# A chunked attention and mixture-of-experts kernel on Trainium2: the value product ahead of the scores in each attention step

## The chip, the cores and the metric

One NeuronCore of one Trainium2 chip runs the whole program. The metric is the device time of one execution in microseconds (us). Before the change the median of three runs is 1189.48 us (1186.12 to 1189.49).

## The reference, cut to what matters

Tokens are 2 batches of 2048 rows of 256 numbers. A layer norm with a per-batch shift and scale feeds an attention with 16 heads of 64 and a window of 128 keys; its output is gated and added. A second modulated layer norm feeds a router and eight experts.

```python
h = layernorm(x) * (1 + ca) + sa
q, k, v = split(h @ Wqkv)                      # 16 heads of 64
scores = (q @ k.T) / 8                         # key j seen by query i if i-127 <= j <= i
x = x + ga * (softmax(scores) @ v).reshape(...) @ Wout
h = layernorm(x) * (1 + cb) + sb
x = x + gb * experts_top2_capacity_640(h)      # relu(h W1 + b1) W2 + b2, gated
```

## The kernel before, in words

**Tiling.** The 4096 tokens are eight chunks of 512 (c = 0 to 7), a chunk is four tiles of 128. In a chunk the attention is cut into 16 units: a pair of heads j times half of the chunk's tiles (two tiles). A unit's scores, probabilities and transposed probabilities are four 128x128 blocks each.

**The pipeline.** A unit passes through five stages on four engines, and each engine has its own hand-written program; only semaphores tie them together:

- `scores` (L568, matmuls on L585), on TensorE, into one of two PSUM tiles `score`;
- on VectorE (DVE) `softmax_step` (L991): `merge` (L967, the window's mask, L976), `invert_sum` (L982, L984), `row_max` (L978, L980), `normalise` (L986, L988), where the sum and the normalisation belong to the unit before; between them ScalarE (ACT) takes the exponentials (`exponentials`, L817, L822);
- `transposes` (L591, L596) on TensorE into the one PSUM tile `pt`, copied by ACT (`copy_probT`, L826, L830);
- `split_keys` (L1230) on GpSimd (POOL), two masked copies (L1237, L1239) into one of two buffers `probT_split`;
- `weighted_values` (L599, L616 and L623) on TensorE, the value product of a pair of heads into the one PSUM tile `pv`. When both halves of the pair are there, ACT takes the high part out (`attn_high`, L832, L836) and DVE the low part (`attn_low`, L999, L1001). In the last chunk this is done for every unit by itself, half as wide (L844, L1096).

**The step.** A chunk is a loop over i = 4 to 19 on every engine. In step i TensorE takes the scores of unit i, the value product of unit i-4, the transposes of unit i-2, and then the projections of q, k or v for the next chunk (`project_qk`, six matmuls of 512 columns on L548; `project_v`, L562). Steps 12, 13, 14 and 16 have a v projection beside the q or k one. Units above 15 belong to the next chunk. Step 5 also has the transposes of the layer norm of chunk c+2. Step 12 has the router's logits (L688), step 15 its counts (L702). After step 19 come four v projections and the output projection (L639). Chunk 6 leaves the projections of pairs 5 to 7 and some of v to chunk 7, so its steps 14 to 19 have none; chunk 7 does them two at a time in its steps 4 to 6, and has no scores after step 15.

**Who waits for whom on TensorE.** `scores` of unit i waits for the exponentials of unit i-2 (`exp_done`), which read the same PSUM tile, and on the first half of a pair for the copy of its q and k out of PSUM (`gen_free`). `weighted_values` of unit u waits for both masked copies (`cur_ready`, `prev_ready`), and as it writes the one tile `pv`, for `attn_low` of the pair before (`attn_lo`), on the first unit of each pair, that is in even steps:

```python
if c == LAST:
    at_least(pe, attn_lo, PAIRS * c + u)
elif part == 0:
    at_least(pe, attn_lo, PAIRS * c + j)
```

On DVE `attn_low` stands at the head of an even step, behind the whole `softmax_step` of the odd step before; on ACT `attn_high` stands in that odd step behind its exponentials. POOL also does the router's modulation: `route_scale` in step 6 (L356), `route_shift` in step 7 (L360), `route_low` (L365) in step 9, each behind that step's `split_keys`; the first waits for DVE's L227 of step 6. From step 16 on it issues the scatters (L1248). In chunks 1 to 6 DVE has `route_top` (L1042 to L1059) after the softmax of step 13, and `route_slots` (L1073 to L1090) behind `attn_low` in step 16.

Of the kernel before, what the change touches and what calls it, by code (L numbers as in the profile page):

```python
# [45 lines left out]
def build(nc, x_in, wqkv_in, wout_in, gate_w, gate_b, w1_in, b1_in, w2_in, b2_in, c_in, wmod_in, out):  # L46
# [22 lines left out]
    with whole:  # L69
# [57 lines left out]
        with attn_stack:  # L127
# [128 lines left out]
            def projections_at(c, i):  # L256

                if c == LAST:
                    return LATE.get(i, [])
                v_tiles = {12: 0, 13: 1, 14: 2, 16: 3}  # L260
                names = [("qk"[i % 2], (i - LAG) // 2)] + ([("v", 0, v_tiles[i])] if i in v_tiles else [])
                return [n for n in names if c != LAST - 1 or n not in LATE_NAMES]
# [14 lines left out]
            def route_at(c):  # L277
                return LAST_AT if c == LAST else ROUTE_AT
# [215 lines left out]
            if True:  # L494
# [27 lines left out]
                def attention_tensor(pe):  # L522
                    def claim(c, name):
                        bank, before = group(c, name)
                        at_least(pe, gen_free[bank], before)
                        return gen[bank], gen_full[bank]
# [64 lines left out]
                    def transposes(c, h):  # L591
                        u = H * c + h
                        pe.wait_ge(norm_ready, u + 1)
                        at_least(pe, probT_ready, u)
                        for b in range(TILES):
                            mm = pe.transpose(pt[:, b, :], prob[:, h % 2, b, :], identf[:])  # L596
                        mm.then_inc(pt_done, 1)
# [108 lines left out]
                    def project(c, name):  # L706
                        cc = c - 1 if c == LAST else c
                        if name[0] == "v":
                            project_v(cc, name[1], [name[2]])
                        else:  # L710
                            project_qk(cc, name)

                    def chunk(c, first, last):
                        at = route_at(c)
                        for i in STEPS:
                            if i < H or not last:
                                scores(c, i)
                            weighted_values(c, i - 4)
                            if i - 2 < H or not last:
                                transposes(c, i - 2)  # L720
                            if last:
                                for name in projections_at(c, i):
                                    project(c, name)
                            if last and i == at["turn"]:
                                route_transposes(c)
                            if not first and i == at["logits"]:
                                route_logits(c)
                            if not first and i == at["counts"]:
                                route_counts(c)
                            if last and i == OUT_AT:  # L730
                                pe.wait_ge(attn_lo, PAIRS * c + PAIRS)
                                early, early_full = claim(c, ("out", 0))
                                project_out_tile(early, 0, range(PAIRS))
                            if last and i == OUT_AT + 1:
                                project_out_tile(early, 1, range(PAIRS)).then_inc(early_full, 1)
                            if last and i == EARLY_AT["turn"]:
                                route_part_transposes(NC)
                            if last and i == EARLY_AT["logits"]:
                                route_logits(NC)
                            if i == 5 and c + 2 < NC:  # L740
                                ln_transposes(c, c + 2, "lnT")
                            if not last:
                                for name in projections_at(c, i):
                                    project(c, name)
                        if not last:
                            for name in projections_after(c):
                                project(c, name)
                            project_out(c)
                            return
                        pe.wait_ge(attn_lo, PAIRS * c + H - 1)  # L750
                        late = [claim(c, ("out", t - 1)) for t in (2, 3)]
                        for t in (2, 3):
                            project_out_tile(late[t - 2][0], t, range(PAIRS - 1))
                        pe.wait_ge(attn_lo, PAIRS * c + H)
                        for t in (2, 3):
                            project_out_tile(late[t - 2][0], t, [PAIRS - 1]).then_inc(late[t - 2][1], 1)
                        route_counts(NC)
                        route_part_transposes(NC + 1)
                        route_logits(NC + 1)
                        route_counts(NC + 1)  # L760
# [850 lines left out]
```

## Time and profile before

| | us |
|---|---|
| median of three runs | 1189.48 |
| lowest, highest | 1186.12, 1189.49 |
| the profiled execution's own time | 1186.38 |
| its span | 1184.7 |
| TensorE busy | 1099.4 |
| VectorE busy | 770.2 |
| ScalarE busy | 661.8 |
| GpSimd busy | 501.2 |

The span runs from the first to the last instruction; 1.7 us of the execution's time lie around it. A chunk of the attention takes 85 us of it, the eight chunks lie between 67 and 722 us, and the experts take the rest. In rows of the timeline the first number is the start of a group of equal instructions and the second the time to the end of the last; TensorE's instructions overlap, so what a part of a step costs is read from start to start.

### The profile page before, as it was taken

The page shows a single profiled execution, that of the slowest core. Times are in us where ns is not written, and L with a number is a line of the kernel's source. Part 1 is how long each engine was busy: PE and PEld are TensorE (multiplying, and loading weights), DVE is VectorE, ACT ScalarE, POOL GpSimd, SP SyncE. Part 2 cuts the span into 40 slices and gives each one's busy share as a digit, 9 for nine tenths or more (in the row PEclk, how much of TensorE's full clock was granted, in tenths as well). Part 3 has the DMA queues.
Part 4 walks back from the last instruction along what each step waited for, and adds up shares of the span by engine and source line. Part 5 has one row for each costly group of instructions (what it writes and reads, how often), then busy time and mean ns, then how long its engine had stood idle before and what let it go on. Part 6 is the DMA issues. An engine that isn't in the chain of part 4 may idle for free.

```text
span 1184.7 us, 25298 instructions
## 1 busy us (share of the span) xinstructions
PE 1099.4 (93%) x9508; PEld 720.3 (61%) x9508; DVE 770.2 (65%) x1687; ACT 661.8 (56%) x1876; POOL 501.2 (42%) x555
## 2 busy tenths in 40 slices
PE   6899999999999999999999874599999999999996
PEld 3355655655655655655656553275858677585865
DVE  6566487586586587585675675376666667666654
ACT  3377566476476476476473753456373746637361
POOL 2134254464364365265344554525243433524342
PEclk9999999999999999999999987699999999999998
DMA  9653000110100011000001021734253444535000
GB/s 330 106 169 132 2 23 20 38 31 16 41 20 26 30 20 37 19 19 31 20 19 50 2 91 36 200 97 94 87 99 113 85 130 112 135 108 84 22 20 9
DMA packets 119627, 80.60 MB, mean 68 GB/s; under 512 B 82770, under 2 KB 110550, under 8 KB 119252
## 3 DMA queue, kind: packets, MB, share of 16 engines
q1 hardware_dynamic: 108756, 57.46, 18.4%
q0 software_dynamic: 10752, 21.54, 6.5%
q8 instruction: 76, 1.25, 0.4%
q14 instruction: 43, 0.35, 0.1%
HBM read 39.49 MB, written 33.78 MB: 62 GB/s over the span
## 4 chain that ended last, share of the span: by engine, by line
PE 76%; DVE 7%; issue 6%; POOL 6%; ACT 3%; DMA 1%; SPq 0%; POOLq 0%; ACTq 0%; DVEq 0%
PE up L1444 18%; PE down L1459 18%; PE gen L548 10%; PE gen L639 6%; PE gen L562 6%; PE score L585 5%; PE pv L616 4%; PE pt L596 4%; PE pv L623 3%; ACT prob L822 2%; POOL probT_split L1237 2%; POOL h L356 1%; POOL probT_split L1239 1%; DVE prob L988 1%; PE gen L647 1%
## 5 line engine op out<-in xcount | busy, mean ns | idle before, releaser
L1503 ACT ACTIVATE hid<-up,b1T 128x512 f16<-128x512 f32 (+1 forms) x192 | 124.4, 648 | 195.3 <-PE up L1444 193.6
L1444 PE MATMUL up<-xT,w 128*128 128x512 f16 (+1 forms) x1152 | 213.1, 346 | 17.2 <-DMA xT<-slot_inputs 17.2
L1459 PE MATMUL down<-w,hid 128*128 128x256 f16 x1920 | 212.2, 273 | 0.0
L1237 POOL TENSOR_SCALAR_AFFINE_SELECT probT_split<-probT 128x512 f32<-128x512 f32 x128 | 98.3, 768 | 262.5 <-ACT probT L830 257.2
L1459 PEld LDWEIGHTS down<-w,hid 128*128 128x128 f16 x1920 | 187.8, 98 | 23.5
L548 PE MATMUL gen<-hT,big 128*128 128x512 f16 x768 | 186.8, 383 | 5.5 <-DVE hT L1197 2.9
L822 ACT ACTIVATE prob<-score,negmax 128x128 f32<-128x128 f32 x512 | 180.9, 374 | 8.0 <-DVE negmax L980 7.9
L1444 PEld LDWEIGHTS up<-xT,w 128*128 128x128 f16 x1152 | 113.4, 98 | 112.6 <-issue 21.1
L1404 POOL DMA_INDIRECT out<-y,tail x80 | 79.9, 998 | 218.5 <-DVE y L1560 206.1
L1531 DVE TENSOR_TENSOR hid<-hid 128x512 f16<-128x512 f32 (+1 forms) x192 | 115.4, 607 | 82.1 <-ACT hid L1505 66.1
L830 ACT ACTIVATE probT<-pt 128x512 f32<-128x512 f32 x128 | 76.6, 598 | 101.3 <-PE pt L596 101.1
L976 DVE COPY_PREDICATED score<-above,score 128x512 f32<-128x512 int32 x112 | 77.2, 690 | 84.3 <-PE score L585 84.3
L1505 ACT ACTIVATE hid<-up,b1T 128x512 f32<-128x512 f32 (+1 forms) x192 | 124.8, 650 | 0.0
L548 PEld LDWEIGHTS gen<-hT,big 128*128 128x128 f16 x768 | 74.3, 99 | 75.9 <-issue 4.7
L585 PE MATMUL score<-k,q 64*64 64x192 f32 (+2 forms) x2048 | 111.6, 331 | 8.0 <-ACT prob L822 5.8
L822 ACT ACTIVATION_READ_ACCUMULATOR prob<-score,negmax 128x1 f32 x512 | 109.9, 215 | 0.0
L616 PE MATMUL pv<-probT_split,v 128*64 128x256 f32 x512 | 84.5, 408 | 24.0 <-issue 7.7
L988 DVE TENSOR_TENSOR prob<-prob,rinv 128x512 f32<-128x512 f32 x128 | 105.4, 823 | 0.0
L1393 POOL DMA_INDIRECT kept<-out,tail x80 | 85.2, 1065 | 47.6 <-issue 30.2
L585 PEld LDWEIGHTS score<-k,q 64*64 64x64 f32 x2048 | 64.9, 133 | 59.5 <-issue 57.3
L562 PE MATMUL gen<-big,hT 128*128 128x512 f16 x384 | 91.3, 384 | 0.0
L1239 POOL TENSOR_SCALAR_AFFINE_SELECT probT_split<-probT 128x512 f32<-128x512 f32 x128 | 86.5, 676 | 0.0
(143 smaller groups left out, 1484.7 us busy)
## 6 DMA issues: line engine op xcount, KB each, us to landing
big<-in_L_ffn_W SPq DMA_DIRECT2D x16, 1024.0 KB, 7.3
slot_inputs<-empty_row SPq DMA_DIRECT2D x80, 129.5 KB, 2.5
out<-x SPq DMA_DIRECT2D x8, 512.0 KB, 2.9
x<-in_L_attn_x SPq DMA_DIRECT2D x1, 3072.0 KB, 22.1
q<-in_L_attn_Wqkv SPq DMA_DIRECT2D x2, 1024.0 KB, 8.0
kept<-out,tail POOLq DMA_INDIRECT x80, 4.8
out<-y,tail POOLq DMA_INDIRECT x80, 2.4
x<-in_L_attn_x SPq DMA_DIRECT2D x2, 512.0 KB, 8.8
```

The lines of the kernel that those rows point to most:

```text
L548: mm = pe.matmul(dst[:], wqkv[:, kd, a, col:col + P], hT[:, cn % 2, kd, b, :], start=(n == 0), stop=(n == 5))
L562: mm = pe.matmul(dst[:], hT[:, cn % 2, kd, a, s * P:(s + 1) * P], wqkv[:, kd, b, 2 * INNER + half * 512:2 * INNER + (half + 1) * 512], sta ...
L585: mm = pe.matmul(dst[lo:lo + HALF, 2 * hd + i, first:lo + P + HALF], q[r:r + DH, j, b * P + lo:b * P + lo + HALF], k[r:r + DH, j, b * P + ...
L616: mm = pe.matmul(pv[r:r + DH, 2 * part * P:(2 * part + 2) * P], v[:, 2 * part + 1, h * DH:(h + 1) * DH], probT_split[:, par, 2 * hd:2 * hd ...
L822: mm = act.activation(prob[:, h % 2, b, :], score[h % 2][:, b, P:], ACT.Exp, bias=negmax[:, h % 2, b:b + 1], accum_out=rowsum[:, h % 2, b: ...
L988: dve.tensor_tensor(prob[:, h % 2], prob[:, h % 2], rinv[:, h % 2, :].unsqueeze(2).to_broadcast([P, TILES, P]), ALU.mult)\
L1237: pool.affine_select(out=probT_split[:, h % 2, :, 1], in_=probT[:, h % 2], pattern=[[0, TILES], [1, P]], compare_op=ALU.is_ge, fill=zero, ...
L1444: mm = pe.matmul(bank[:, 0:size], w1[:, par, kd, a, ft * P:(ft + 1) * P], xT[:, par, b * KD + kd, lo:lo + size], start=(i == 0), stop=(i = ...
L1459: mm = pe.matmul(down[n][:, s, :], hid[:, ft, a, t * P:(t + 1) * P], w2[:, par, ft, b, :], start=(i == 0), stop=(i == 3 * FT - 1))
L1503: act.activation(hid[:, ft, 0, lo:lo + size], up[ft % 4][:, 0:size], ACT.Relu, scale=1 / W_SCALE, bias=bias).then_inc(hid_hi, 1)
L1505: act.activation(hid32[:, k_ % 4, 0:size], up[ft % 4][:, 0:size], ACT.Relu, scale=1 / W_SCALE, bias=bias).then_inc(up_out, 1)
L1531: dve.tensor_tensor(hid[:, ft, 1, lo:lo + size], hid32[:, k_ % 4, 0:size], hid[:, ft, 0, lo:lo + size], ALU.subtract).then_inc(hid_ready, 1)
```

## The change: what it does, and the diff

In the step loop of TensorE's program the call for the value product of unit i-4 moves ahead of the call for the scores of unit i. The programs of the other four engines, the waits, the tiles and the data are the same.

```diff
--- before.py
+++ after.py
@@ -713,9 +713,9 @@
                     def chunk(c, first, last):
                         at = route_at(c)
                         for i in STEPS:
+                            weighted_values(c, i - 4)
                             if i < H or not last:
                                 scores(c, i)
-                            weighted_values(c, i - 4)
                             if i - 2 < H or not last:
                                 transposes(c, i - 2)
                             if last:
```

TensorE's order before, from the scores of an odd step in the middle of a chunk to the value product of the next, even step (each helper's first matmul carries its waits):

```order
L585 MATMUL score<-k,q 64x192 [waits exp_done]
L585 MATMUL score<-k,q 64x192 x7
L616 MATMUL pv<-probT_split,v 64x256 [waits cur_ready,prev_ready]
L616 MATMUL pv<-probT_split,v 64x256
L623 MATMUL pv<-probT_split,v 64x128 x4
L596 MATMUL pt<-identf,prob 128x128 [waits probT_ready,norm_ready]
L596 MATMUL pt<-identf,prob 128x128 x3
L548 MATMUL gen<-hT,big 128x512 [waits gen_free1]
L548 MATMUL gen<-hT,big 128x512 x5
L585 MATMUL score<-k,q 64x192 [waits exp_done,gen_free0,gen_free1]
L585 MATMUL score<-k,q 64x192 x7
L616 MATMUL pv<-probT_split,v 64x256 [waits attn_lo,cur_ready,prev_ready]
```

And with the change, from the same scores to the same value product:

```order
L585 MATMUL score<-k,q 64x192 [waits exp_done]
L585 MATMUL score<-k,q 64x192 x7
L596 MATMUL pt<-identf,prob 128x128 [waits probT_ready,norm_ready]
L596 MATMUL pt<-identf,prob 128x128 x3
L548 MATMUL gen<-hT,big 128x512 [waits gen_free1]
L548 MATMUL gen<-hT,big 128x512 x5
L616 MATMUL pv<-probT_split,v 64x256 [waits attn_lo,cur_ready,prev_ready]
```

Between the odd step's scores and the wait on `attn_lo` stood two groups of value products, transposes, projections and scores; now transposes and one projection stand there, since the odd step's value product is done before its scores and the even step's scores come behind the wait.

The last chunk on TensorE before, steps 11 and 12, where every value product waits on `attn_lo`:

```order
L596 MATMUL pt<-identf,prob 128x128 [waits probT_ready,norm_ready]
L596 MATMUL pt<-identf,prob 128x128 x3
L585 MATMUL score<-k,q 64x192 [waits exp_done]
L585 MATMUL score<-k,q 64x192 x7
L616 MATMUL pv<-probT_split,v 64x256 [waits gen_free0,attn_lo,gen_free1,cur_ready,prev_ready]
L616 MATMUL pv<-probT_split,v 64x256
L623 MATMUL pv<-probT_split,v 64x128 x4
```

The same place with the change:

```order
L596 MATMUL pt<-identf,prob 128x128 [waits probT_ready,norm_ready]
L596 MATMUL pt<-identf,prob 128x128 x3
L616 MATMUL pv<-probT_split,v 64x256 [waits gen_free0,attn_lo,gen_free1,cur_ready,prev_ready]
L616 MATMUL pv<-probT_split,v 64x256
L623 MATMUL pv<-probT_split,v 64x128 x4
L585 MATMUL score<-k,q 64x192 [waits exp_done]
L585 MATMUL score<-k,q 64x192 x7
```

The scores of unit 12 went from ahead of this wait to behind it. The orders of DVE and ACT are the same before and after.

## Rows read from the trace of the kernel before

**Rows 1.** The page, part 1: busy us (share of span) xinstructions, each engine.
```profile
PE 1099.4 (93%) x9508; PEld 720.3 (61%) x9508; DVE 770.2 (65%) x1687; ACT 661.8 (56%) x1876; POOL 501.2 (42%) x555
```

**Rows 2.** Busy us by stretch, chunk 3: window, length, then each engine's busy (x instructions).
```profile
319.00:404.00 85.00, 82.60 (x814) 51.16 (x808) 59.05 (x145) 52.01 (x180) 41.96 (x48) 1.00 0.09 26
```

**Rows 3.** Waits in total, of L616 and of L1001: us, times, longest us.
```profile
PE pv L616 <- POOL probT_split L1239: 7.2, 14, 1.0
PE pv L616 <- DVE attn L1001: 4.9, 8, 1.2
...
DVE attn L1001 <- ACT attn L836: 0.2, 1, 0.2
```

**Rows 4.** Timeline of TensorE, chunk 3, step 9 and start of 10: start, us.
```profile
339.53 0.88 PE L585 MATMUL score<-k,q 64*64 64x192 f32 x16
340.58 0.65 PE L616 MATMUL pv<-probT_split,v 128*64 128x256 f32 x4 [0.18 <-POOL probT_split L1239]
...
341.60 0.66 PE L596 MATMUL pt<-identf,prob 128*128 128x128 f32 x4
342.10 1.46 PE L548 MATMUL gen<-hT,big 128*128 128x512 f16 x6
343.48 0.88 PE L585 MATMUL score<-k,q 64*64 64x192 f32 x16
344.30 0.65 PE L616 MATMUL pv<-probT_split,v 128*64 128x256 f32 x4
```

**Rows 5.** Timeline of VectorE, the same steps 9 and 10.
```profile
340.48 0.70 DVE L976 COPY_PREDICATED score<-above,score 128x512 f32<-128x512 int32 x1 [0.51 <-PE score L585]
341.66 0.18 DVE L984 RECIPROCAL rinv<-rowsum 128x4 f32<-128x4 f32 x1 [0.49 <-ACT prob L822]
...
342.33 0.68 DVE L988 TENSOR_TENSOR prob<-prob,rinv 128x512 f32<-128x512 f32 x1
342.93 0.68 DVE L1001 TENSOR_TENSOR attn<-pv,attn 128x512 f16<-128x512 f32 x1
...
345.42 0.68 DVE L976 COPY_PREDICATED score<-above,score 128x512 f32<-128x512 int32 x1
346.01 0.17 DVE L984 RECIPROCAL rinv<-rowsum 128x4 f32<-128x4 f32 x1
```

**Rows 6.** Timeline, chunk 3, steps 7 and 8: the chain over POOL.
```profile
332.58 2.36 POOL L356 TENSOR_TENSOR h<-h,modrow 128x1024 f32<-128x1024 f32 x1 [3.86 <-DVE h L227]
335.94 0.63 POOL L1239 TENSOR_SCALAR_AFFINE_SELECT probT_split<-probT 128x512 f32<-128x512 f32 x1
336.62 0.65 PE L616 MATMUL pv<-probT_split,v 128*64 128x256 f32 x4 [0.60 <-POOL probT_split L1239]
```

**Rows 7.** Timeline, chunk 3, steps 11 to 14.
```profile
350.14 1.52 DVE L988 TENSOR_TENSOR prob<-prob,rinv 128x512 f32<-128x512 f32 x1
...
352.47 0.65 PE L616 MATMUL pv<-probT_split,v 128*64 128x256 f32 x4 [0.68 <-POOL probT_split L1237]
...
359.40 0.18 DVE L984 RECIPROCAL rinv<-rowsum 128x4 f32<-128x4 f32 x1 [0.49 <-ACT prob L822]
...
362.83 0.68 DVE L1001 TENSOR_TENSOR attn<-pv,attn 128x512 f16<-128x512 f32 x1
...
363.66 0.65 PE L616 MATMUL pv<-probT_split,v 128*64 128x256 f32 x4 [0.51 <-DVE attn L1001]
```

**Rows 8.** Timeline of TensorE, chunk 6, step 18.
```profile
628.45 0.65 PE L616 MATMUL pv<-probT_split,v 128*64 128x256 f32 x4 [1.15 <-DVE attn L1001]
```

**Rows 9.** Timeline of TensorE, chunk 7, steps 5 and 12.
```profile
652.56 0.88 PE L585 MATMUL score<-k,q 64*64 64x192 f32 x16 [0.73 <-issue]
687.68 1.12 PE L616 MATMUL pv<-probT_split,v 128*64 128x256 f32 x4 [2.80 <-issue]
```

**Rows 10.** Busy us by stretch; the third last column is the granted clock.
```profile
628.00:632.00 4.00, 2.55 (x34) 1.79 (x36) 3.08 (x7) 2.49 (x13) 3.40 (x5) 1.00 0.16 57
686.00:688.00 2.00, 0.32 (x2) 0.32 (x4) 1.93 (x14) 0.10 (x2) 0.05 (x1) 0.79 1.09 377
```

## The prediction

> **What bounds the kernel now.** I began with the page's busy times: TensorE is busy for 93% of the span [rows 1]. The busy times by stretch say that this holds inside the attention too: 82.6 of 85 us in chunk 3, at the full granted clock [rows 2]. So a step of the attention lasts as long as TensorE's own work, and what matters is how near the other engines are behind. The table of waits answers that: the value product L616 waits 14 times for POOL and 8 times for DVE, 1.2 us at most [rows 3]. They are short, but they show two chains that only just arrive. The timeline then gives the lengths, all from start to start [rows 4]: scores S 0.82 (343.48 to 344.30), value product V 1.02 (340.58 to 341.60), transposes T 0.50, one projection Q 1.38 us. A plain step is 3.72 us. (A measurement of this kernel can tell 0.3%, 3.6 us, from no change.)
>
> **The change, part by part.** It removes and adds no instruction on any engine, and no DMA; each of 124 pairs of S and V is swapped. TensorE's work stays the same, so without waits it costs 0. The swap has two effects on waits. V comes 0.82 us earlier against a producer that has not moved. And S comes 1.02 us later in its step, with everything that DVE does behind it.
>
> *The even steps, a plain pair.* V of an even step waits for `attn_low`, which stands behind the odd step's whole softmax on DVE. From S of the odd step the chain is [rows 5]: 0.95 to the merge (339.53 to 340.48), 0.59 merge to reciprocal (345.42 to 346.01), 0.67 reciprocal to normalisation, 0.60 to `attn_low`, 0.68 for that, and 0.15 from its end to TensorE's start (363.51 to 363.66) [rows 7]: 3.64 us. Before, the reciprocal came later, 2.13 us after S, since it waited for ACT's exponentials; that made 4.23 us. TensorE covered it with S, V, T, Q and the next S, 4.54 us: 0.3 us of slack, no wait. Now the exponentials stand where they stood in the step while S comes 1.02 later, so the merge sets the reciprocal and the chain is 3.64. But TensorE has only S, T and Q in front of the wait, 2.70 us. **The wait is 0.94 us**, and nothing takes it back, as the next such chain starts behind it. Behind the waiting V stand S of its own step, T and Q; DVE idles for S. If this wait were gone, POOL would be late next.
>
> *Step 8.* V waited 0.60 us for POOL's copies, which were late because L356 began only behind DVE's L227 [rows 6]. L227 moves with the softmax of step 6: merge-bound, the reciprocal comes 1.02 + 0.95 + 0.59 = 2.56 us after the step's start instead of 2.13, 0.43 later, and POOL with it. V begins 0.43 later than before, and S, which was done during the wait, now comes behind: 0.43 + 0.82, **1.2**. Step 9's V waits for POOL as before (0.18, [rows 4]): 0.
>
> *Step 12.* On DVE the normalisation of step 11 takes 1.52 instead of 0.68 us [rows 7], beside a POOL instruction. The chain is 3.64 + 0.84, TensorE's cover 2.70: a wait of 1.8 where 0.68 was [rows 7]. (The row names POOL, but those copies belong to the next unit; `attn_low` ended just before.) **1.1.**
>
> *Step 14.* The router's small instructions lie between reciprocal and `attn_low`: 359.40 to 363.51, 4.11 us [rows 7]. The chain from S is 0.95 + 0.59 + 4.11 + 0.15 = 5.80. The cover is S, T, Q and a v projection of 1.3: 4.0. Wait 1.8, where 0.51 was, and S used to be done inside it: 1.8 less 0.51 is **1.2 to 1.3**, as the chain also lost 0.58 of waiting for ACT, V's 1.02 now lying ahead of S. I take 1.24.
>
> *Steps 10, 16, 18.* Plain pairs at 10 and 18: 0.94 each. Ahead of step 16 the counts (0.36 us) cover some: 0.58. Step 6 has the layer norm's transposes as cover: 0.
>
> Chunks 1 to 5: 1.2 + 0.94 + 1.1 + 1.24 + 0.58 + 0.94 = 6.0 us each, 30.2. **Chunk 0** has no router: 0.94 before steps 8, 10, 16 and 18, and step 12's 1.1: 4.9. **Chunk 6**: 1.2 + 0.94 + 0.94 + 1.24 up to step 14. From there it has no projections, and waits of up to 1.15 us already [rows 8]; walking the pairs in the same way gives +1.3 and +0.5, and 0.6 back at step 19, where the scatters on POOL set the time: 5.5. **Chunk 7** hands over in every step. Its steps 4 to 7 come out even: S waited 0.73 us for the copy of its k [rows 9], three times, and now V lies in that wait. Steps 8, 9 and 11 cost 1.5, 0.7 and 0.7. In step 12 V waits 2.80 us [rows 9] and S, issued ahead of that wait until now, comes behind: 1.8, and its softmax then holds the V of step 13: 1.1. At step 16 the long DVE chain starts from an S 1.02 later: 1.0. With 0.3 won before: 6.5. This walk is the roughest term.
>
> Sum 30.2 + 4.9 + 5.5 + 6.5 = **47 us**. The experts come after and are only shifted: 0, unless the shift moves the last DMA. On the profiled execution's 1186.38 us this gives 1233.5; the median of the runs is 3.1 above it, so 1236.5.
>
> *A cost the trace does not show*: the new neighbours on TensorE (V behind a projection, S behind V, T behind S). The nearest rows are the overlaps of neighbours now, 0.06 to 0.08 us (S lasts 0.88, the next starts after 0.82; Q 1.46 and 1.38) [rows 4]. Three seams a step in 64 odd steps (even ones wait anyway): at most 15 us more or less. I take 0, since the tile shapes change as often as before, and keep both ends.
>
> **The rivals.**
> *Only the waits already there grow.* If DVE's chain of a plain pair fits after all (it would have to be 0.94 us shorter), the terms of 0.94 and 0.58 fall away: 12.3 in chunks 1 to 5, 3.8 in chunk 0, 1.9 in chunk 6, about 18. Time: 1218. For it: the chain had 0.3 of slack, so my two lengths differ by small numbers. Against: the five spans of which it is made would have to be read too long together.
> *Hidden.* Every V finds its inputs at the step's start: 1189.5. The four waits of a chunk that the trace already has speak against it.
> *Faster.* One mechanism: V 0.82 us earlier lets ACT's L836 and so `attn_low` end earlier, and the waits on DVE go. It decides if L1001 waits for L836. It did so once, for 0.2 us [rows 3]; L1001 is held by DVE's own queue. Price if true: 4.9 us of L1001's waits [rows 3], step 12's five of 0.68 [rows 7], three of 0.73 [rows 9]: 10.5 us, 1179.
> *The clock falls.* After the wait of 2.80 us in step 12 of chunk 7 the value product took 1.12 instead of 0.65 us [rows 9], and the granted clock of that stretch was 0.79 on the way to half, the 1.2 GHz level [rows 10]. In chunk 6, with TensorE idle for 1.4 of 4 us in pieces, it stayed at 1.00, 2.4 GHz [rows 10]. My new waits of 1.8 to 1.9 us at steps 8, 12 and 14 lie between the two. If each cost a V and an S at half rate, 1.8 us, 20 times, the time is 1236.5 + 36 = 1272. The Trainium skill (TensorE: Matmul & The Clock Gate, Part 1) has the half rate as the gate's default that only activity lifts; by that rule this rival is the danger in a change that only adds idle time, and the trace agrees in its 2.80 us wait. I hold it unlikely, since dense work stands on both sides of each wait.
>
> **How the numbers follow.** Forecast 0.74, only existing waits 0.13, clock 0.06, hidden 0.04, faster 0.03. The range 1212 to 1258 holds the forecast with most of its seam costs (15 either way) and 7 more for the walks of chunks 6 and 7, and the second case; the clock, hidden and faster cases are left out. Slower by over 0.3%: 0.93; within: 0.04; faster: 0.03.
>
> **What would show it.** In the profile of the changed kernel L616's waits for DVE L1001 should grow from 8 to some 45, of 0.9 to 1.9 us; a chunk of 85 us should last 91; L976 should start 0.95 us after its scores and the reciprocal 0.6 after it, no longer waiting for ACT in odd steps; V of step 8 should wait about 1.9 us for L1239. TensorE's busy time should stay within a few us of 1099 and the clock of chunks 0 to 6 at 1.00. I am wrong if plain pairs still take 7.4 us, or if the waits are there and the end has not moved.

## The result, and the profile after

The changed kernel takes 1260.28 us (median of four runs, 1257.7 to 1262.96), beside 1188.9 for the kernel before on the same chip (1186.12 to 1189.49): a ratio of 1.061, 95% interval 1.0594 to 1.0625. The change costs 71 us. The forecast was 47 us (1236.5), and the range ended at 1258. The sign and the mechanism were as predicted, the size was not.

The page of the changed kernel, its span and part 1:

```profile
span 1258.3 us, 25298 instructions
...
PE 1112.6 (88%) x9508; PEld 727.5 (58%) x9508; DVE 775.1 (62%) x1687; ACT 661.7 (53%) x1876; POOL 520.4 (41%) x555
```

TensorE has 13 us more of busy time than in [rows 1], the span has 74 more: some 60 us are new idle time of TensorE. By stretch, a chunk in the middle (chunk 3; the columns are those of [rows 2], the third last is the granted clock):

```profile
336.00:428.50 92.50, 82.70 (x802) 51.19 (x800) 59.50 (x144) 51.73 (x180) 44.48 (x48) 1.00 0.08 24
```

The work is that of [rows 2], at the same full clock; the chunk lasts 92.5 us where it had 85. The waits in total (us, times, longest us) name what TensorE waits for:

```profile
PE pv L616 <- DVE attn L1001: 43.6, 29, 3.0
...
PE pv L616 <- POOL probT_split L1239: 13.5, 8, 2.0
PE pv L616 <- POOL probT_split L1237: 11.5, 7, 2.5
```

In [rows 3] the value product waited 4.9 us for `attn_low` in 8 waits; now it is 43.6 in 29. The timeline of chunk 3, steps 8 to 10, is the plain pair of the prediction (start, us; lines of other instructions left out):

```profile
360.68 0.65 PE L616 MATMUL pv<-probT_split,v 128*64 128x256 f32 x4 [1.90 <-POOL probT_split L1239]
...
365.42 0.88 PE L585 MATMUL score<-k,q 64*64 64x192 f32 x16
...
366.36 0.69 DVE L976 COPY_PREDICATED score<-above,score 128x512 f32<-128x512 int32 x1 [1.17 <-PE score L585]
366.97 0.17 DVE L984 RECIPROCAL rinv<-rowsum 128x4 f32<-128x4 f32 x1
...
367.70 0.68 DVE L988 TENSOR_TENSOR prob<-prob,rinv 128x512 f32<-128x512 f32 x1
...
368.30 0.68 DVE L1001 TENSOR_TENSOR attn<-pv,attn 128x512 f16<-128x512 f32 x1
...
369.13 0.65 PE L616 MATMUL pv<-probT_split,v 128*64 128x256 f32 x4 [0.95 <-DVE attn L1001]
```

Scores to merge 0.94, merge to reciprocal 0.61, then 0.73, 0.60, 0.68 and 0.15 to TensorE's start: 3.71 us where 3.64 was forecast, and a wait of 0.95. Step 8 waits 1.90 for POOL. So the steps of the prediction can be read one by one. What the delay against the old order grows by, read at the start of each step's transposes (step 4 of chunk 7, 0.87 us, is counted with chunk 6):

| | forecast, us | measured, us |
|---|---|---|
| chunk 0 | 4.9 | 6.8 |
| chunk 1 | 6.0 | 9.3 |
| chunks 2, 3 and 5, each | 6.0 | 7.7 |
| chunk 4 | 6.0 | 7.2 |
| chunk 6 | 5.5 | 14.1 |
| chunk 7 | 6.5 | 12.7 |
| sum | 47 | 73.1 |

| step of chunk 3 | 8 | 9 | 10 | 12 and 13 | 14 | 16 | 18 |
|---|---|---|---|---|---|---|---|
| forecast | 1.2 | 0 | 0.94 | 1.1 | 1.24 | 0.58 | 0.94 |
| measured | 1.30 | -0.24 | 1.02 | 1.11 | 1.76 | 1.04 | 1.72 |

Before the attention and in the experts the kernels differ by under 2 us.

The 13 us of added busy time are no added work; the instructions are the same 9508. They lie in three chunks, and these are the ones in which the granted clock fell: by the busy times of each chunk TensorE has 1.9 us more in chunk 1 (clock 0.98 where it was 1.00), 4.9 more in chunk 6 (0.94, was 1.00) and 5.5 more in chunk 7 (0.85, was 0.95), and at most 0.4 more in each of the others. So up to 12 of the 73 us are the slower clock. The changed kernel's four executions fit this: at mean clocks of 0.969, 0.967, 0.966 and 0.964 their spans are 1256.0, 1258.3, 1258.8 and 1261.3 us.

### The profile page after: what moved, and what is told of

The parts are those of the page before. It is cut to its first block, busy times and chain, and to the rows that moved or that the text cites. A ratio compares the mean times of both kernels' runs of the same rounds, so it can differ in the third digit from the quotient of the medians.

```text
span 1258.3 us, 25298 instructions
## 1 busy us (share of the span) xinstructions
PE 1112.6 (88%) x9508; PEld 727.5 (58%) x9508; DVE 775.1 (62%) x1687; ACT 661.7 (53%) x1876; POOL 520.4 (41%) x555
## 4 chain that ended last, share of the span: by engine, by line
PE 72%; DVE 13%; issue 6%; POOL 6%; ACT 2%; DMA 1%; SPq 0%; POOLq 0%; ACTq 0%; DVEq 0%
PE up L1444 17%; PE down L1459 16%; PE score L585 7%; PE gen L548 7%; PE gen L639 6%; PE gen L562 5%; PE pv L616 5%; PE pv L623 4%; PE pt L596 3%; DVE prob L988 3%; DVE score L976 2%; DVE negmax L980 2%; POOL probT_split L1237 1%; DVE attn L1001 1%; POOL probT_split L1239 1%
## 5 line engine op out<-in xcount | busy, mean ns | idle before, releaser
L1444 PE MATMUL up<-xT,w 128*128 128x512 f16 (+1 forms) x1152 | 212.9, 346 | 18.5 <-DMA xT<-slot_inputs 17.1
L1237 POOL TENSOR_SCALAR_AFFINE_SELECT probT_split<-probT 128x512 f32<-128x512 f32 x128 | 95.4, 746 | 295.7 <-ACT probT L830 289.4
L616 PE MATMUL pv<-probT_split,v 128*64 128x256 f32 x512 | 85.9, 412 | 83.9 <-DVE attn L1001 43.6
L585 PE MATMUL score<-k,q 64*64 64x192 f32 (+2 forms) x2048 | 115.8, 341 | 5.5 <-ACT prob L822 5.5
L988 DVE TENSOR_TENSOR prob<-prob,rinv 128x512 f32<-128x512 f32 x128 | 116.7, 912 | 0.0
L616 PEld LDWEIGHTS pv<-probT_split,v 128*64 128x64 f32 x512 | 27.2, 137 | 135.3 <-issue 96.0
L1239 POOL TENSOR_SCALAR_AFFINE_SELECT probT_split<-probT 128x512 f32<-128x512 f32 x128 | 105.2, 822 | 0.0
```

The costliest lines, as they stand in the source:

```text
L585: mm = pe.matmul(dst[lo:lo + HALF, 2 * hd + i, first:lo + P + HALF], q[r:r + DH, j, b * P + lo:b * P + lo + HALF], k[r:r + DH, j, b * P + ...
L616: mm = pe.matmul(pv[r:r + DH, 2 * part * P:(2 * part + 2) * P], v[:, 2 * part + 1, h * DH:(h + 1) * DH], probT_split[:, par, 2 * hd:2 * hd ...
L988: dve.tensor_tensor(prob[:, h % 2], prob[:, h % 2], rinv[:, h % 2, :].unsqueeze(2).to_broadcast([P, TILES, P]), ALU.mult)\
L1239: pool.affine_select(out=probT_split[:, h % 2, :, 0], in_=probT[:, h % 2], pattern=[[0, TILES], [-1, P]], compare_op=ALU.is_gt, fill=zero, ...
L1444: mm = pe.matmul(bank[:, 0:size], w1[:, par, kd, a, ft * P:(ft + 1) * P], xT[:, par, b * KD + kd, lo:lo + size], start=(i == 0), stop=(i = ...
```

## The experiments

In all kernels but the two compared above, the DMA transposes (L518 and the two that load `xT`) are plain copies of the same bytes, so that the router and the experts work on tokens that were not transposed; the attention is unchanged. Of each the span and the growth by step are compared with those of the first, ctrl1, whose only edit this is. "Forecast" is what the prediction's working gives. The growth by step repeats well (chunks 0 to 5 to 0.1 us between the two kernels with the whole change); a span or a median moves by several us between executions (the kernel before: 1186.6 to 1194.6 us beside the second run below), and ctrl1 ran on another chip than the rest, so a difference of a few us between two spans shows nothing by itself. The edits shown are cut to what matters.

**ctrl1: are the copies worth anything?**

> The kernel before, without its DMA transposes: plain copies of the same bytes take their place (the router's input of chunks 1 to 6 and the experts' input are then untransposed, so the routing and the output are other numbers). It is the control for all runs below. Every theory: the attention is as before (85 us a chunk, from the first scores to the last output projection within 2 us of before), the whole within 20 us of 1188.9, most likely less, since the first load of the experts' input is shorter.

```diff
-sp.dma_start(xT[:, par].bitcast(U16), xbuf[...], transpose=True)
+sp.dma_start(xT[:, par]..., xbuf[...].rearrange("(t p) m -> p t m", p=P))
```

1185.13 us (8 runs) beside 1185.71, ratio 0.9995 (0.9983 to 1.0006); span 1183.5. The copies are worth nothing.

**swap_plain_copy: the change on that base.**

> The changed kernel, without its DMA transposes as in the control (the router's and the experts' input are untransposed copies). Every theory: the same 71 us above its control as the changed kernel is above before (65 to 76). If it is not, the transposes had a part in it.

1260.05 us beside 1189.12, ratio 1.0588 (1.049 to 1.0685); span 1256.0, 72.5 over ctrl1 (65 to 76 expected), with the same growth by step as above to 0.1 us in chunks 0 to 5. The cost is the change's own. Chunk 6 costs 14.8 and chunk 7 10.5 here.

**even_steps and odd_steps: one half of the swaps.** The value product goes first only in even steps (the one that waits for `attn_low` moves past its own step's scores), or only in odd ones (the scores of the odd step, which start DVE's chain, move back).

```diff
+values_first = i % 2 == 0        # odd_steps: i % 2 == 1
+if values_first:
+    weighted_values(c, i - 4)
 if i < H or not last:
     scores(c, i)
-weighted_values(c, i - 4)
+if not values_first:
+    weighted_values(c, i - 4)
```

> Value product first in even steps only (no DMA transposes). Theory 1 (hand-off: the even step's value product stands behind attn_low, and attn_low behind the odd step's softmax): the scores of the odd step keep their place, the chain from them to attn_low keeps its 4.23 us, TensorE has scores, value product, transposes, projection ahead of the wait, 3.72: 0.5 us a plain pair, 1.0 to 1.3 at steps 8, 12 and 14, about 4.5 to 5 us a chunk and up to 12 in the last: 38 to 47 us above the control. Theory 2 (each swapped step costs the same, as scores come late to DVE and ACT): half, 35 us. Theory 3 (POOL: the value product is early for its two masked copies, at steps 8, 12, 14): all of it, 65 to 71 us.

> Value product first in odd steps only (no DMA transposes). Theory 1 (hand-off): from the odd step's scores TensorE has scores, transposes, projection and the next scores ahead of the wait, 3.52 us, against a chain of 3.71: 0.2 us a plain pair, 0.6 where the normalisation runs beside POOL's copies, step 8's wait for POOL grows by 0.4; chunks 1 to 5 cost 1.5 to 2.5 us each, the whole 12 to 25 us above the control, so that even steps and odd steps alone (37) do not add up to the 72 of both by a like share. Theory 2 (each swapped step costs the same): 36 us, as even steps alone.

even_steps: 1224.62 us, ratio 1.029 (1.0197 to 1.0384), span +37.3. odd_steps: 1218.84 us, ratio 1.0253 (1.0228 to 1.0278), span +34.3. The totals don't bear theory 1 out: 37.3 lies just under its 38 to 47, 34.3 well over its 12 to 25, and both are nearer to the 35 and 36 of theory 2, by which each swapped step costs the same. It is the steps that speak against theory 2: with the even steps swapped, chunk 3 grows by 1.31 at step 8, 0.52 at step 10 and 0.17 at step 16. A plain pair in chunk 0 grows by 0.52 in the one run (0.5 expected) and by 0.59 to 0.70 in the other (0.2 expected), 1.40 with both. Odd steps alone also cost time at other places than the whole change does: in chunks 1 to 5 step 9 grows by 0.8 and step 10 by 1.6 to 1.8, where the whole change has -0.24 to 0.09 and 1.02 (0.94 in chunk 4; chunk 1 has 0.67 at step 9, by the clock). In chunk 3 the value product of step 9 waits 0.99 for POOL's copies, and that of step 10 waits 1.52 for `attn_low`, behind a normalisation (L992 here) that takes 2.06 us beside POOL's `route_low`:

```profile
352.56 2.06 POOL L365 TENSOR_TENSOR packed<-h,packed 128x1024 f16<-128x1024 f32 x1 [1.64 <-ACT packed L854]
353.10 2.06 DVE L992 TENSOR_TENSOR prob<-prob,rinv 128x512 f32<-128x512 f32 x1
```

So the halves have costs of their own, and that these add up to the whole (71.6 of 72.5) is luck. What decides between the theories is the next run.

**low_in_odd: the wait itself.** The changed order, with `attn_low` taken from the head of the even step to the odd step before, right behind the reciprocal (chunks 0 to 6).

```diff
-for stage, unit, there in ((merge, i, new), (invert_sum, i - 1, old), (row_max, i, new),
+low = i >= 5 and i % 2 == 1 and not last
+for stage, unit, there in ((merge, i, new), (invert_sum, i - 1, old), (attn_low, (i - 5) // 2, low), (row_max, i, new),
                            (normalise, i - 1, old)):
...
-if i >= 6 and i % 2 == 0 and not last:
-    attn_low(c, (i - 6) // 2)
...
-attn_low(c, PAIRS - 1)       # behind step 19
```

> The changed order, but in chunks 0 to 6 DVE takes attn_low in the odd step right behind the reciprocal, not at the head of the next even step (no DMA transposes). Theory 1: the chain from the scores of the odd step falls to 0.95 + 0.61 + 0.12 + 0.68 + 0.15 = 2.5 us, under the 2.70 that TensorE has; what is left is step 8's wait for POOL (1.3 us, seven times) and the last chunk's 12: 20 to 27 us above the control. Theory 2: nothing about the scores changes, 71 us. Theory 3: the waits at steps 8, 12 and 14 stay, at least 50 us.

1204.1 us, ratio 1.0118 (1.0035 to 1.0201), span 1202.0: 54 of the 72.5 us are gone, and 18.5 are left where theory 1 had 20 to 27. Of the 43 us of waits for `attn_low` (L1001) one of 0.9 is left; in chunk 0 no step grows any more. What stays is step 8 (+1.32, POOL), 0.74 at step 10 (there L988 takes 2.40 us beside POOL's `route_low` and the transposes wait 0.68 for it), 4.9 in chunk 6, and chunk 7 with 10.4, which the edit leaves alone. The scores come to DVE as late as in the changed kernel, so theory 2 is out. The chain by way of `attn_low` is the cause of the greater part, shown by taking it away.

**split_late: DVE and POOL beside each other.** In the changed kernel the normalisation L988 and a masked copy often slow each other. The timeline of chunk 0, first of ctrl1, then of the changed kernel, a plain pair of each:

```profile
127.75 0.68 DVE L988 TENSOR_TENSOR prob<-prob,rinv 128x512 f32<-128x512 f32 x1
128.13 0.79 POOL L1237 TENSOR_SCALAR_AFFINE_SELECT probT_split<-probT 128x512 f32<-128x512 f32 x1 [2.33 <-ACT probT L830]
...
128.88 0.63 POOL L1239 TENSOR_SCALAR_AFFINE_SELECT probT_split<-probT 128x512 f32<-128x512 f32 x1
```

```profile
130.60 0.63 POOL L1237 TENSOR_SCALAR_AFFINE_SELECT probT_split<-probT 128x512 f32<-128x512 f32 x1 [3.34 <-ACT probT L830]
130.72 1.06 DVE L988 TENSOR_TENSOR prob<-prob,rinv 128x512 f32<-128x512 f32 x1
131.19 1.08 POOL L1239 TENSOR_SCALAR_AFFINE_SELECT probT_split<-probT 128x512 f32<-128x512 f32 x1
131.70 0.68 DVE L1001 TENSOR_TENSOR attn<-pv,attn 128x512 f16<-128x512 f32 x1
...
132.53 0.65 PE L616 MATMUL pv<-probT_split,v 128*64 128x256 f32 x4 [1.33 <-DVE attn L1001]
```

L988 begins while L1237 runs and takes 0.38 us more; the next copy, L1239, begins while L988 runs and takes 0.45 more. That 0.38 is in TensorE's wait: 1.33 instead of 0.95. The edit makes the copies wait for the next unit's normalisation:

```diff
-waits = [(probT_ready, u + 1)]
+waits = [(probT_ready, u + 1), (norm_ready, min(u + 2, H * NC))]
```

> The changed order, but POOL's two masked copies of a unit also wait for the normalisation of the next unit, so that they no longer run beside it (no DMA transposes). Contention theory (the part of the excess over the forecast comes from DVE's normalisation and POOL's copies slowing each other): L988 falls back from a mean of 0.91 to about 0.82 us and L1239 from 0.82 to 0.68, and the chain of each even step is 0.4 us shorter where it was slowed: 10 to 18 us less than the changed order, 53 to 61 above the control. Rival (the excess is the last two chunks and the clock): within 3 us of the changed order. A third way: POOL's copies, 0.7 us later, keep the value product waiting, and it is slower than the changed order.

1246.88 us, ratio 1.0477 (1.0391 to 1.0563), span 1245.5: 10.5 less, at the lower end of the 10 to 18 expected. The groups of instructions in the changed order (swap_plain_copy), and with the edit:

```profile
L988 DVE TENSOR_TENSOR prob<-prob,rinv 128x512 f32<-128x512 f32 x128 | 115.1, 900 | 0.0
...
L1239 POOL TENSOR_SCALAR_AFFINE_SELECT probT_split<-probT 128x512 f32<-128x512 f32 x128 | 104.8, 818 | 0.0
```

```profile
L988 DVE TENSOR_TENSOR prob<-prob,rinv 128x512 f32<-128x512 f32 x128 | 97.8, 764 | 0.0
...
L1239 POOL TENSOR_SCALAR_AFFINE_SELECT probT_split<-probT 128x512 f32<-128x512 f32 x128 | 81.4, 636 | 0.0
```

The means fall from 900 to 764 ns and from 818 to 636 ns. The plain pair of chunk 0 grows by 1.02 instead of 1.40, step 16 of chunk 3 by 0.67 instead of 1.04: the overlap cost 0.38 a time, on the path. But the 10.5 us are not all of this kind. About 1.1 lie before the attention and 1.6 behind its last transposes; chunks 0, 1 and 6 gain 1.4, 2.7 and 3.4 (in the latter two the clock, too, falls at fewer places), and chunks 2 to 5 together only 0.6, since the later copies make new waits for L1237 (27.4 us in 21 waits) and step 18 stays at 1.65 to 1.87.

**last_chunk: chunk 7 alone has the new order.**

```diff
+values_first = last
```

> Value product first in the last chunk only (no DMA transposes). The forecast had 6.5 us for this chunk, the changed kernel shows 12.3 there. If that cost is the chunk's own (every unit hands pv over, and the long DVE stretches of steps 11 and 15 leave TensorE idle long enough for its clock to fall): 11 to 14 us above the control. If part of it was carried over from chunk 6 (its late end, its slow clock): 6 to 9.

1196.87 us beside 1188.74, ratio 1.0068 (1.0043 to 1.0093), span 1194.5: 8.1 us in the medians, 11.0 in the spans over ctrl1. These two leave the 11 to 14 and the 6 to 9 both open; by the steps, which repeat best, the chunk grows by 9.6 with nothing changed ahead of it. That is most of the 10.5 to 12.7 it costs in the whole change, so the greater part is the chunk's own; forecast were 6.5.

**scatters_at_19: why does step 18 cost 1.72?** The timeline of the changed kernel, chunk 3, step 17:

```profile
407.41 0.88 PE L585 MATMUL score<-k,q 64*64 64x192 f32 x16
407.69 0.99 POOL L1248 DMA_INDIRECT slot_inputs<-packed,send  x1 [0.17 <-PE pv L623]
...
408.22 0.66 PE L596 MATMUL pt<-identf,prob 128*128 128x128 f32 x4
...
409.04 0.70 DVE L976 COPY_PREDICATED score<-above,score 128x512 f32<-128x512 int32 x1 [3.61 <-PE score L585]
...
409.76 0.60 ACT L830 ACTIVATE probT<-pt 128x512 f32<-128x512 f32 x1 [0.79 <-PE pt L596]
...
411.81 0.65 PE L616 MATMUL pv<-probT_split,v 128*64 128x256 f32 x4 [1.64 <-DVE attn L1001]
```

DVE had been idle for 3.61 us, and still the merge began 1.63 after the scores' start, not 0.94; ACT's copy began 1.54 after the transposes' start, not 0.69. A scatter of POOL lies beside the scores. This is so in steps 17 and 18 of each of chunks 1 to 5 (the merge 1.52 to 1.63 behind the scores' start), and nowhere in the trace of before, where the scatters of these steps began behind the scores in chunks 2 to 5; in chunk 1 two of them ran into the scores by 0.16 and 0.62 us, with the merge at 0.95. The edit:

```diff
-if not first and at["slots"] <= i < at["slots"] + TILES:
+if last and at["slots"] <= i < at["slots"] + TILES:
     scatter(c, [i - at["slots"]])
+if not first and not last and i == at["slots"]:
+    scatter(c, [0])
+if not first and not last and i == at["slots"] + 3:
+    scatter(c, [1, 2, 3])
```

> The changed order with plain copies, and in chunks 1 to 6 the scatters L1248 of steps 17 and 18 issued behind those of step 19. It asks why step 18 grew by 1.70 us where a plain pair grows by 1.02. In steps 17 and 18 of the changed kernel a scatter is on POOL while the scores are on TensorE, and the merge L976 starts 1.63 us after the scores' start instead of 0.95. Theory 1 (the scatter beside the scores makes their result late on DVE): without it the merge starts at 0.95 again, step 18 grows by 1.0 instead of 1.70, and the chunks 1 to 5 are 0.7 us shorter each; span about 1252, 3 to 4 under the changed order's 1256.0. Theory 2 (the lateness comes from TensorE's own new order at that place): the merge is late as before, step 18 still grows by 1.7, span 1256 or more, as six scatters now stand ahead of the next chunk's first masked copies.

1249.39 us, ratio 1.0544 (1.0519 to 1.0569), span 1249.7, 6.3 less. By the ratios a gain is not clear, as 1.0544 lies within the 1.049 to 1.0685 of swap_plain_copy; the steps have to tell. The same step:

```profile
406.76 0.88 PE L585 MATMUL score<-k,q 64*64 64x192 f32 x16
407.71 0.69 DVE L976 COPY_PREDICATED score<-above,score 128x512 f32<-128x512 int32 x1 [2.93 <-PE score L585]
408.27 0.60 ACT L830 ACTIVATE probT<-pt 128x512 f32<-128x512 f32 x1
...
409.05 1.06 DVE L988 TENSOR_TENSOR prob<-prob,rinv 128x512 f32<-128x512 f32 x1
...
410.86 0.65 PE L616 MATMUL pv<-probT_split,v 128*64 128x256 f32 x4 [1.33 <-DVE attn L1001]
```

The lateness is gone in all ten places (the merge of step 17 is back at 0.95): it comes with the scatters of steps 17 and 18. But theory 1, the scatter beside the scores, is not enough for a cause. In this same run the scatter of step 19 begins 0.29 us behind the scores' start, as in step 17 above, and the merge comes at 0.95, in each of chunks 1 to 5:

```profile
415.48 0.88 PE L585 MATMUL score<-k,q 64*64 64x192 f32 x16
...
415.77 0.99 POOL L1248 DMA_INDIRECT slot_inputs<-packed,send  x1 [0.16 <-issue]
...
416.43 0.69 DVE L976 COPY_PREDICATED score<-above,score 128x512 f32<-128x512 int32 x1 [1.31 <-PE score L585]
```

What else has to come together stays open. The price was misjudged too. Step 18 grows by 1.40 and not by 1.0, because L988 now meets L1237 and takes 1.06; the scatter's net cost is 0.3 there. So chunks 1 to 5 gain 1.5 us together. Chunk 6 grows by 9.0 where swap_plain_copy has 14.8, with its step 14 at 1.76 instead of 3.32 and at the full clock; chunk 7 gives 2 back (12.7 where it had 10.5), and 1.1 lie behind the attention. Whether the clock held in chunk 6 because of the edit or by chance, one trace cannot tell.

**swap_low_all: the last chunk's `attn_low_part` in its own step too.**

```diff
+(attn_low_part, i - 4, low_part)     # in softmax_step, ahead of the row max; low_part = i >= LAG and last
-if last and i >= 5:
-    attn_low_part(c, i - 5)
...
-attn_low_part(c, H - 1)              # behind step 19
```

> The changed order with plain copies, with attn_low of the pair ahead of the row max in the odd step, and in the last chunk attn_low_part in its own step instead of the next. Without the last part the span was 1202.0, and chunk 7 still cost 12 us against the old order. Theory 1 (chunk 7's cost is the value product's wait for attn_low_part at the head of the next step): most of the 12 goes, span 1190 to 1193. Theory 2 (there the scores now stand behind waits of the value product that come from its own scores of the step before, through row max, exponentials, POOL's copies, whichever step attn_low_part stands in): the 12 stays but for the 2.3 that the same edit brought in the old order, span about 1199 to 1200. By both it stays slower than the old order with the same edits (1176.9).

1191.67 us, ratio 1.0055 (1.0038 to 1.0071), span 1191.0: 11 less than low_in_odd (8 less by the medians, each beside its own kernel before). The steps of chunk 7 take 3.9 us less than in ctrl1, where low_in_odd had 10.4 more; 2.6 us are given back behind step 19. Theory 1's 1190 to 1193 held: chunk 7's cost was the wait for `attn_low_part` as well.

**old_low_in_odd and old_low_all: `attn_low` moved up in the order of before,** one instruction later than above (between row max and normalisation).

> The order of before, with DVE's attn_low in the odd step between row maximum and normalisation, chunks 0 to 6 (no DMA transposes). Theory 1: the waits of before for attn_low go: 1.2 us in each of chunks 1 to 5, 0.4 in chunk 0, 2.3 in chunk 6: 8 to 9 us under the control (low_in_odd showed -0.74 at step 12 and -0.57 at step 14 against before). Against it: the normalisation, 0.6 us later in odd steps, could keep the transposes waiting: then 0 to 4 under.

> As the run before it, and also in the last chunk, where attn_low of each unit moves from the head of the next step to its own step, ahead of the normalisation (no DMA transposes). Theory 1: the waits of 2.8 us (step 12) and 4.3 us (step 16) of the last chunk stood behind route_top and add_attention, which attn_low now precedes: 3 to 6 us under the run before it. If DVE's own work is the bound of these steps, only up to 1 us.

1180.72 us, ratio 0.9932 (0.9914 to 0.9951), and 1178.79 us (1178.42 to 1179.78), ratio 0.9918 (0.9899 to 0.9937), beside 1188.74 for the kernel before. The first is 8.0 us under it in the medians, as theory 1 had it (8 to 9), but only 4.3 under ctrl1 in the span, and the steps are nearer to the latter: chunks 1 to 5 gain 0.6 to 1.0 us each where 1.2 were expected (in most of them 0.74 at step 12 and 0.57 at step 14, of which step 13 gives 0.31 back), and chunk 6 gains nothing of its 2.3. The second was to be 3 to 6 us under the first and is 1.9 under it (2.3 in the span). Still it beats both kernels: the one before by 10 us in the medians (7.5 to 12 by the interval; 6.6 in the span, 1176.9 against ctrl1's 1183.5), and the new order with the like places by 14 us of span. In its chunk 7 V of step 12 no longer waits the 2.80 us of [rows 9] and that step's growth is -3.64; part of this comes back as a wait of 4.3 us for POOL at step 17.

Not tried: a second `pv` tile, which should take the wait for `attn_low` away in any order, if one fits beside the PSUM tiles that the kernel has (two `score`, `pt`, `pv`, two `gen`).

## Why the prediction was wrong in its size, and where it was right

The steps that failed are four terms of the sum, and the clock, which was left out of it. Of the 26 us missed (73.1 against 47), 11.2 lie in chunks 0 to 5: there the chain was priced with DVE's lengths unchanged, where L988 took 0.38 to 0.44 more beside POOL's copies (5.6 us), the merge came late in step 17 (3.5), and the clock fell once (1.6). 8.6 lie in chunk 6 and 6.2 in chunk 7, where the walks were too short and TensorE ran at the lower clock for part of the time (4.9 and 5.5 us more busy time).

**Right.** What bounds the kernel, and the two moves (V against a producer that stays, S and DVE's chain 1.02 later). The plain pair: 0.94 forecast, 0.95 of idle time and 1.02 of growth. Step 8: 1.2 forecast, 1.30; its wait is 1.90 on L1239 as foretold. Steps 12 and 13: 1.1 against 1.11. Step 9, taken as 0, gave 0.24 back: its V was no longer held by POOL. The reciprocal stands 0.61 behind the merge and waits no more for ACT. The waits for L1001 are 29 and not some 45, as some are now put down to POOL, but they last 43.6 us. The experts are only shifted. The seams between TensorE's neighbours cost 0, as taken: 82.70 us of work in chunk 3 against 82.60, and steps 5, 7, 11 and 15 of chunks 0 to 5, which have no new wait, grow by 0.00. That low_in_odd takes away 54 of 72.5 us shows that the mechanism is this one.

**Wrong: "from S of the odd step the chain is ... 0.60 to `attn_low`".** I took DVE's durations from [rows 5], 0.68 for L988, and moved them 1.02 us against POOL as if they did not depend on what POOL does. The trace of before had the warning in [rows 7]: 1.52 "beside a POOL instruction", which I used for step 12 alone. It even had the very pair, one step earlier in chunk 3:

```profile
346.68 0.64 POOL L1237 TENSOR_SCALAR_AFFINE_SELECT probT_split<-probT 128x512 f32<-128x512 f32 x1
346.74 1.12 DVE L988 TENSOR_TENSOR prob<-prob,rinv 128x512 f32<-128x512 f32 x1
```

The swap brings L988 and the masked copies of the unit before to the same moment, for 0.38 to 0.44 us in every even pair of chunk 0 and ahead of steps 14 and 16 of the others: chunk 0 6.8 instead of 4.9, and step 14's 1.76 and step 16's 1.04 are the forecast 1.24 and 0.58 plus 0.44 or 0.38 and the 0.07 by which the normalisation now stands further behind the reciprocal (0.73 instead of 0.67). Over chunks 0 to 5 the slower L988 is 5.6 us (0.38 times 4, and 0.82 times 5), of a miss of 26 in all eight.

**Wrong: "steps 10, 16, 18 ... 0.94 each".** Step 18 measured 1.72. The late merge makes 0.69 of the difference, the 0.07 the rest: some 3.5 us in five chunks. (Without the scatter 0.38 of it would have stood there in the other way.) I had named POOL's queue only where TensorE waits for it, not for what its scatters lie beside.

**Wrong: chunk 6, 5.5 against 14.1.** "Step 6 has the layer norm's transposes as cover" holds in chunks 1 to 5; chunk 6 has none to make, and its step 6 grew by 1.33. Its steps 14 to 19 have no projections, so that nothing stands ahead of a late V, and the clock came in:

```profile
669.84 1.12 PE L616 MATMUL pv<-probT_split,v 128*64 128x256 f32 x4 [2.27 <-DVE attn L1001]
```

```profile
670.00:672.00 2.00, 2.00 (x16) 1.36 (x19) 0.00 (x0) 0.00 (x0) 0.00 (x0) 0.50 0.04 8
```

V takes 1.12 instead of 0.65, and the granted clock of the stretch is 0.50, the 1.2 GHz level. Step 14 grew by 3.33 (1.24 forecast), step 18 by 2.63, with S at 1.56 us there. The clock also fell in steps 8 and 9: they grew by 2.68 together, where 1.2 was forecast and scatters_at_19 has 1.06. scatters_at_19 has step 14 at 1.76 and step 18 at 0.89, at the full clock.

**Wrong: chunk 7, 6.5 against 12.7.** "This walk is the roughest term" was true, and the 15 us that I gave the whole sum were meant for the seams. Step 8 cost 2.6 to 3.3 in the two kernels with the whole change where 1.5 was walked (2.0 in last_chunk), step 9 1.2 where 0.7, step 12 2.5 where 1.8, step 13 2.6 (1.3 in swap_plain_copy) where 1.1, step 16 1.8 to 2.0 where 1.0. S took 1.56 us, the lower clock, in steps 8 and 12. That swap_low_all turns the chunk's cost into a gain of 3.9 shows that it hangs on `attn_low_part`; how the rest of the miss splits between the clock and the length of the chains no run shows.

**The clock** was given a chance of 0.06 as a rival by itself. It came neither as the rival had it (20 places, 36 us) nor not at all: at one place in chunk 1 (step 8, 1.6 us with step 9), three in chunk 6, several in chunk 7. "Dense work stands on both sides of each wait" did not keep it up: in chunk 1 it fell behind the 1.90 us wait of step 8. The mean granted clock is 0.967, where before and ctrl1 have 0.979. By the steps of chunks 1 and 6 it adds some 6.5 us (1.6; 2.68 less 1.06; 3.33 less 1.76; 2.63 less 0.89), and by TensorE's busy time up to 12 with chunk 7. No run changes the clock alone, so this share is read from the traces and not shown by an experiment. A range made of one case's errors did not hold a part of another case.

**The range.** Every one of the four errors went up, and but for chunk 6's step 6 they have one thing in common: I kept the durations of DVE, POOL and TensorE as they were and shifted them. Where a change makes the pieces of several engines meet anew, lengths may well grow (here the mean of L988 went from 0.82 to 0.91 us, that of L1239 from 0.68 to 0.82), and the range should have reached further on that side.

## What to carry to other kernels

Before a producer's chain is put ahead of work that covers it, count from the chain's start to the wait, and what the waiting engine has in between; here the cover fell from 4.54 to 2.70 us and the chain was 3.64, and the difference was paid at every plain pair. Then look what else will now run at the same moment on engines that slow each other, and price each such instruction at the length that the trace already shows for it beside that neighbour. And when a wait is at the end of such a chain, first try to move the waited-for instruction up in its own queue: `attn_low` some places earlier gave 7 to 10 us in the old order (span, medians), and 65 of the 72.5 in the new.

## What the runs showed of the hardware that I had not expected

**DVE's normalisation and POOL's instructions took turns.** L988, 0.68 us alone, began at 130.72 while L1237 ran to 131.23, and ended 0.55 behind that end; L1239, 0.63 alone, ended 0.49 behind L988. Beside POOL's long L365 a normalisation took 2.40 us in low_in_odd:

```profile
344.94 2.40 DVE L988 TENSOR_TENSOR prob<-prob,rinv 128x512 f32<-128x512 f32 x1
```

L1001, which reads `pv` from PSUM and one tile from SBUF, never did (minimum, median and maximum over 56, in ns):

```profile
L1001 DVE TENSOR_TENSOR attn<-pv,attn x56: 677/684/684, 74.8 to 694.4; 128x512 f16<-128x512 f32 x56
```

nor did L980, which reads PSUM alone (660 to 692 ns). The Trainium skill (SBUF — State Buffer, "SBUF: two separate sides") says that a VectorE instruction with two SBUF inputs and a GpSimd one that reads SBUF hold a shared port pair in turn, each for its whole length. L988 has two SBUF inputs and the masked copy reads `probT` there, and the trace agrees but for 0.13 to 0.14 us: L988 grew by 0.38 where L1237 ran on for 0.51, L1239 by 0.45 where L988 ran on for 0.59.

**Work of TensorE reached DVE and ACT late in the steps of some scatters,** by 0.58 to 0.69 us (the merge) and 0.74 to 0.87 (ACT's copy) in chunks 1 to 5, at ten regular places, and not once the scatters had moved. Overlap alone does not bring it: five scatters of step 19 in scatters_at_19 lie beside the scores in the same way as those of step 17 here, with the merge at 0.95. The ends of matmuls are modelled in this profile, so it does not tell whether the matmuls themselves or only the signal of them came late. Both are open.

**The same wait does not always cost the clock.** V of step 8 waits 1.90 us for L1239 in chunk 1 and in chunk 3. In chunk 3 the scores behind it ran at the full rate (0.81 to the transposes' start); in chunk 1 they took 1.56, and the granted clock from 175.0 to 176.5 us was 0.50:

```profile
173.91 0.65 PE L616 MATMUL pv<-probT_split,v 128*64 128x256 f32 x4 [1.90 <-POOL probT_split L1239]
...
174.93 1.56 PE L585 MATMUL score<-k,q 64*64 64x192 f32 x16
```

The order of TensorE's work ahead of both waits is the same. So a wait's length alone did not settle it here, and a forecast of single places would have to be a chance for each.
